# Self attention of a two-block network on one core: the causal mask moved from TensorE to VectorE and GpSimd, and the value products placed two units behind

## What is computed

```python
h = _layer_norm(x, ln1_g, ln1_b)
q, k, v = jnp.split(h @ w_qkv, 3, axis=-1)            # each B, S, 16, 16
scores = jnp.einsum('bqhd,bkhd->bhqk', q, k) * hd ** (-0.5)
causal = jnp.tril(jnp.ones((S, S), bool))
scores = jnp.where(causal, scores, jnp.finfo(scores.dtype).min)
attn = jax.nn.softmax(scores, axis=-1)
o = jnp.einsum('bhqk,bkhd->bqhd', attn, v).reshape(B, S, D)
x_resid = x + o @ w_o
```

## Time and profile before

| | |
|---|---|
| median of 3 runs | 2925.25 us (2921.18 to 2925.60) |
| span of the profiled execution | 2927.1 us, 1.85 us above the median |
| busy over the span | PE 2456.1, DVE 1872.1, POOL 1530.9, ACT 1332.9 us |
| maxima of set 0 | from 1228.3 to 1269.9 us |
| the seven sets with maxima beside them | from 1269.9 to 1563.1 us |
| last set | to 1592.2 us |

### The profile page before, as it was taken

The page is one execution under the profiler, slowest core; times in us unless marked ns, Lnnn a source line. Parts: engine busy times, 40 slices in busy tenths (PEclk is TensorE's granted clock), DMA queues, the critical chain, the costliest instruction groups (busy, mean ns, idle before and its releaser), DMA issues. The chain is left out here.

```text
span 2927.1 us, 26112 instructions
## 1 busy us (share of the span) xinstructions
PE 2456.1 (84%) x8044; PEld 1106.1 (38%) x8044; DVE 1872.1 (64%) x2521; ACT 1332.9 (46%) x2087; POOL 1530.9 (52%) x1340
## 2 busy tenths in 40 slices
PE   7989989889897788688888549999588989778978
PEld 3333323333332233333333338888332333223322
DVE  2999999999999933466663400000239999994334
ACT  4656466565664433345555212222056565542333
POOL 2999999999999811500000230000439999982010
PEclk9999999999999999899999669999689999999989
DMA  4031230321203000612310324444230320300000
GB/s 186 1 115 47 94 117 1 122 70 55 115 1 115 0 21 17 141 24 33 45 23 1 138 106 181 177 175 175 79 155 1 116 94 24 115 1 20 0 9 29
DMA packets 72193, 215.12 MB, mean 73 GB/s; under 512 B 14044, under 2 KB 39271, under 8 KB 53495
## 3 DMA queue, kind: packets, MB, share of 16 engines
q1 hardware_dynamic: 65380, 180.85, 18.9%
q10 hardware_dynamic: 3602, 24.22, 2.5%
q0 software_dynamic: 3072, 8.39, 0.9%
HBM read 187.80 MB, written 25.43 MB: 73 GB/s over the span
## 5 line engine op out<-in xcount | busy, mean ns | idle before, releaser
L895 POOL TENSOR_TENSOR s_dbu<-s_dx,s_bc 128x512 f32<-128x512 f32 x768 | 967.8, 1284 | 47.9 <-DVE s_psum L561 44.1
L480 PE MATMUL s_psum<-s_hc,ident 128*128 128x512 f32 x1536 | 832.2, 632 | 181.2 <-DVE s_hc L581 170.2
L764 ACT ACTIVATE s_psum<-s_dt,s_a_neg 128x512 f32<-128x512 f32 x768 | 521.6, 688 | 590.5 <-DVE s_hc L581 589.5
L480 PEld LDWEIGHTS s_psum<-s_hc,ident 128*128 128x128 f32 x1536 | 257.9, 192 | 695.2 <-DVE s_hc L581 505.4
L581 DVE TENSOR_TENSOR s_hc<-s_psum,s_bc 128x512 f32<-128x512 f32 x624 | 419.8, 673 | 0.6 <-PE s_psum L480 0.4
L561 DVE TENSOR_TENSOR_SCAN s_psum<-s_psum,s_state,s_dbu 128x512 f32<-128x512 f32 x312 | 395.1, 1277 | 18.5 <-ACT s_psum L764 12.7
L561 DVE TENSOR_TENSOR_SCAN s_psum<-s_psum,s_dbu 128x512 f32<-128x512 f32 x312 | 381.3, 1222 | 22.0 <-ACT s_psum L764 13.8
L1968 ACT ACTIVATE s_probs<-s_banks 128x512 f32<-128x512 f32 (+3 forms) x384 | 169.2, 493 | 149.5 <-PE s_banks L1693 107.0
L2381 POOL DMA_INDIRECT s_rows_in<-moe_out_rows,s_place x32 | 30.6, 957 | 357.0 <-DMA moe_out_rows<-s_ys 347.5
L2360 ACT ACTIVATE s_hidden<-s_banks,s_w 128x256 f32<-128x256 f32 x184 | 77.1, 470 | 300.9 <-PE s_banks L2183 300.9
L163 POOL TENSOR_TENSOR s_pair<-s_res 128x512 f32<-128x512 f32 x4 | 5.0, 1265 | 386.1 <-issue 384.6
(11 more groups left out here) (306 smaller groups left out, 3320.6 us busy)
## 6 DMA issues: line engine op xcount, KB each, us to landing
s_bc<-fwd_rows SPq DMA_DIRECT2D x64, 1024.0 KB, 4.7
s_bc<-m_rows SPq DMA_DIRECT2D x32, 1024.0 KB, 4.7
s_w<-in_moe_w SPq DMA_DIRECT2D x23, 1028.0 KB, 7.2
s_w<-in_moe_w ACTq DMA_DIRECT2D x23, 1024.0 KB, 5.5
qk_parts<-s_parts SPq DMA_DIRECT2D x48, 128.0 KB, 1.9
s_stack_q<-qk_parts SPq DMA_DIRECT2D x48, 128.0 KB, 4.5
s_stack_k<-qk_parts SPq DMA_DIRECT2D x48, 128.0 KB, 7.6
moe_in_rows<-s_zero SPq DMA_DIRECT2D x1, 5888.0 KB, 18.8
```

The costliest lines, as they stand in the source:

```text
L480: pe.matmul(psum[:, SCANS + block_no % 2, :], consts["ident"][:], hc[:, unit % PRODUCTS, :], start=(n == 0), stop=(n == NS - 1)).then_inc( ...
L764: act.activation(psum[:, unit % SCANS, :], dt[:, g % 2, i // NS, :], ACT.Exp, scale=a_neg[CHUNKS[g][0]][:, i:i + 1]).then_inc(decay_ready, 1)
L895: pool.tensor_tensor(dbu[:, unit % TERMS, :], dx[:, g % 2, i // NS, :], bc[:, 2 * n, :], ALU.mult)\
```

## The change

The mask matmuls are gone. Maxima tiles on the diagonal are reduced with `tensor_tensor_reduce`, which adds a mask tile from SBUF (`late`, now 512 columns: 384 of zeros that POOL writes, and the triangle) and takes the maximum in one statement, writing the sum back to the bank. The exponentials on the diagonal are taken without a mask, and POOL sets the forbidden ones to zero (`cut_late`, one `affine_select` for the four heads of a unit, 128 columns each); the value products of such a unit wait for POOL (`causal`) instead of ACT. Value products come two units behind the weights instead of one (`BEHIND`), so those of units 10 and 11 come in the next set, and `probs` is three units deep (`HELD`). `turn_out`, `copy_out` and `norm_heads` move accordingly.

```diff
+HELD, BEHIND = 3, 2
...
-        probs = s.sb("probs", [P, 2 * HH, CH])
+        probs = s.sb("probs", [P, HELD * HH, CH])
...
+        DIAGONAL = [t // 4 == half for t, half in UNITS]
+        def cut(q, u):
+            return q * sum(DIAGONAL) + sum(DIAGONAL[:u + 1])
...
-            sp.dma_start(late[:], dram["tri"]).then_inc(late_loaded, 16)
+            sp.dma_start(late[:, CH - P:CH], dram["tri"]).then_inc(late_loaded, 16)
...                                        # max_tile
-                if t // 4 == half:
-                    mm = pe.matmul(bank[:, w - P:w], consts["identb"][:], lateb[:, 0, :], start=False,
-                                   stop=True, skip_group_check=True)
                 mm.then_inc(max_ready, 1)
...                                        # weight_tile
-                mm = pe.matmul(bank[:, 0:w], stack_k[:, q % SLOTS, j, t * P:(t + 1) * P],
-                               stack_q[:, q % SLOTS, j, q0:q0 + w], start=True, stop=True)
-                if t // 4 == half:
-                    mm = pe.matmul(bank[:, 0:P], consts["identb"][:], lateb[:, 1, :], start=False, stop=True,
-                                   skip_group_check=True)
-                mm.then_inc(scored, 1)
+                pe.matmul(bank[:, 0:w], stack_k[:, q % SLOTS, j, t * P:(t + 1) * P],
+                          stack_q[:, q % SLOTS, j, q0:q0 + w], start=True, stop=True).then_inc(scored, 1)
...                                        # mix_heads
-                pe.wait_ge(exp_done, q * TILES + (u + 1) * HH)
+                if DIAGONAL[u]:
+                    pe.wait_ge(causal, cut(q, u))
+                else:
+                    pe.wait_ge(exp_done, q * TILES + (u + 1) * HH)
...                                        # the order on PE
-                    if u:
-                        mix_heads(q, u - 1)
-                    if q and u == 2:
+                    if u >= BEHIND:
+                        mix_heads(q, u - BEHIND)
+                    elif q:
+                        mix_heads(q - 1, NU + u - BEHIND)
+                    if q and u == 4:
                         turn_out(q - 1, 1)
-                    if u == 7:
+                    if u == 8:
                         turn_out(q, 0)
                     if q + 1 < NSETS and u == 10:
                         turn_max(q + 1)
-                mix_heads(q, NU - 1)
+            for u in range(NU - BEHIND, NU):
+                mix_heads(NSETS - 1, u)
...                                        # maxima, on DVE
-                dve.tensor_reduce(to, banks[:, i % 2, 0:w], AX.X, ALU.max).then_inc(max_read, 1)
+                if t // 4 == half:
+                    dve.tensor_tensor_reduce(banks[:, i % 2, 0:w], banks[:, i % 2, 0:w], late[:, CH - w:CH], 1.0, -3e38,
+                                             ALU.add, ALU.max, to).then_inc(max_read, 1)
+                else:
+                    dve.tensor_reduce(to, banks[:, i % 2, 0:w], AX.X, ALU.max).then_inc(max_read, 1)
...                                        # DVE, among the maxima of the next set
-                        if q and k == 17:
+                        if q and k == 26:
                             norm_heads(q - 1, 1)
-                        if k == 42:
+                        if k == 46:
                             norm_heads(q, 0)
...                                        # exp_tile and copy_out, on ACT
-                if j == 0 and unit >= 2:
-                    act.wait_ge(pv_done, unit - 1)
+                if j == 0 and unit >= HELD:
+                    act.wait_ge(pv_done, unit - HELD + 1)
-                    if q and u == 1:
+                    if q and u == 3:
                         copy_out(q - 1, 1)
-                    if u == 5:
+                    if u == 6:
                         copy_out(q, 0)
...                                        # new, on POOL, for every diagonal unit of every set
+            def cut_late(q, u):
+                pool.wait_ge(exp_done, q * TILES + (u + 1) * HH)
+                diagonal = probs[:, u % HELD * HH:(u % HELD + 1) * HH, 0:P]
+                pool.affine_select(out=diagonal, in_=diagonal, pattern=[[0, HH], [1, P]], compare_op=ALU.is_ge,
+                                   fill=0.0, base=0, channel_multiplier=-1).then_inc(causal, 1)
+            pool.memset(late[:, 0:CH - P], 0.0).then_inc(late_made, 1)
```

More of the change, by code:

```diff
@@ L1473, in self_attention @@
         w_o = s.sb("w_o", [P, KD, D])
-        late = s.sb("late", [P, 2, P])
-        lateb = s.sb("lateb", [P, 2, P], BF16)
+        late = s.sb("late", [P, CH])
         parts = s.sb("parts", [P, 2, PARTS, 4, CH], BF16)
@@ L1501, in self_attention @@
         pads_made, ones_made, late_made = s.sem("pads_made"), s.sem("ones_made"), s.sem("late_made")
+        causal = s.sem("causal")
         ready, split, split3 = s.sem("ready"), s.sem("split"), s.sem("split3")
@@ L1706, in mix_heads @@
                     mm = pe.matmul(banks[j * VW:(j + 1) * VW, 4 + half, CH - w:CH], v[:, b * QT + t, g * HH + j, :],
-                                   probs[:, u % 2 * HH + j, 0:w], start=(t == 0), stop=(t == 4 * half + 3))
+                                   probs[:, u % HELD * HH + j, 0:w], start=(t == 0), stop=(t == 4 * half + 3))
                 mm.then_inc(pv_done, 1)
@@ L1863, in _ @@
             scale_h(3)
-            dve.wait_ge(late_loaded, 16)
-            dve.tensor_copy(lateb[:], late[:]).then_inc(late_made, 1)
             for c in range(2, NCH):
@@ L1868, in _ @@
                     remainder(c, m)
+            dve.wait_ge(late_loaded, 16)
+            dve.wait_ge(late_made, 1)
             for k in range(TILES):
@@ L1964, in exp_tile @@
                 unit = q * NU + u
-                if j == 0 and unit >= 2:
-                    act.wait_ge(pv_done, unit - 1)
+                if j == 0 and unit >= HELD:
+                    act.wait_ge(pv_done, unit - HELD + 1)
                 act.wait_ge(scored, i + 1)
-                act.activation(probs[:, u % 2 * HH + j, 0:w], banks[:, WEIGHT_BANKS[i % len(WEIGHT_BANKS)], 0:w], ACT.Exp)\
+                act.activation(probs[:, u % HELD * HH + j, 0:w], banks[:, WEIGHT_BANKS[i % len(WEIGHT_BANKS)], 0:w], ACT.Exp)\
                    .then_inc(exp_done, 1)
@@ L2022, in _ @@
                 scale_res(c)
+            for q in range(NSETS):
+                for u in range(NU):
+                    if DIAGONAL[u]:
+                        cut_late(q, u)
 NSL = 256
@@ L2646, in layout @@
     tri = np.where(np.arange(P)[None] > np.arange(P)[:, None], np.float32(-1e30), np.float32(0))
-    a["tri"] = np.stack([tri, tri.T], 1)
+    a["tri"] = tri
     a["lns"] = np.stack([cols(i[f + n], KD) for n in ("ln1_g", "ln1_b", "ln2_g", "ln2_b")], 1)
```

1 line of the change is left out of this document (removed).

## The result

The changed kernel took 2929.86 us (median of 14 runs, 2925.75 to 2936.60), the kernel before on the same chip 2925.09 us (14 runs, 2919.12 to 2928.88): a ratio of 1.0021, 95% interval 1.0013 to 1.0029. It became slower, by about 6 us by the ratio and 4.8 by the two medians. I had forecast 2920.4, a gain; the number that I gave for rival (c), PE's clock, was 2929.5.

The account below looks back on a forecast made before the run. A chain of hand-overs bounds the sets, no engine being full. Six full sets −1.7, first set −2.3, first maxima −0.9, last set 0: −4.9 us from the median, 2920.4; range 2909 to 2933, the forecast's own 2916 to 2925.

Parts of the forecast that it names:

- rival (c): PE's clock: with less PE work, a second low stretch in each set costs about 1.3 us; 2929.5 us, chance 0.14.
- Sum of a set: Net of all terms in a full set of the attention: −2.46 + 1.12 + 0.57 + 0.48 = −0.29 us.
- Mask matmuls: 64 a set on PE; taking them out of the chain of hand-overs saves 2.46 us a set.
- Masked maxima: On DVE, each masked tile ends 0.08 us later; 14 such delays a set on the path: +1.12 us.
- rival (a): The masked maximum is delivered free, within the 682 ns of a reduction: −13.4 us, 2911.9 us, chance 0.22.
- (b): One delay swapped for another: 0.16 us a masked tile, +3.6 us, 2928.9 us, no measurable change; chance 0.16.
- (d): The masked maximum runs at the scan's rate: +4.7 us a set instead of +1.12, 2945 us, chance 0.08.
- Value products two behind: More product time in front of `turn_max` (+0.15 us) and low clock in units 0 and 1 (0.42): +0.57 a set.
- `norm_heads`: Moved to tile 26, it delays unit 5's fifth maximum by 0.61 us; its old place cost 0.13: net +0.48.
- POOL's mask: Eight a set, 0.65 us each, hidden until over 3 us; exposed only at the end.
- First maxima: 16 groups of three before the sets: −1.5 us from mask delays and issue, 8 × 0.08 back, −0.9 in all.
- Last set and end: After the last weight tile three units' products follow, one waiting for POOL: +0.9 us, offset by gains, put at 0.

Follow-up runs that it names:

- The halves alone: Kernel before with only the maxima masked on DVE: ratio 0.9979; changed kernel with the maxima masked by TensorE as before: ratio 0.9998.
- only_pool: Changed kernel with the maxima masked by TensorE matmuls and plain reductions as before, the rest of the change kept: 2931.78 us, ratio 0.9998.
- after_warm: Changed kernel with ten extra unread 512-column matmuls on TensorE in front of its wait for the row: 2918.17 us, ratio 0.9954.
- before_warm: Kernel before with ten extra unread 512-column matmuls on TensorE in front of its wait for the row: 2921.84 us, ratio 0.9968.
- behind2: Kernel before with only the change's order (value products two units behind, exponentials three deep, `norm_heads` moved), all mask matmuls kept: 2935.86 us, ratio 1.0007.

## Why the prediction was wrong, step by step

**The step that failed is the clock: rival (c), to which I gave 0.14, and a sum with no term for it.** I wrote that the windows "show 1.00 in every other stretch, which speaks against it". They show the kernel with its masks; what had to be asked is what holds the clock up there, and the change removes just that. One of my signs of being wrong came: a clock of 0.91 over the sets. The mechanism of (c) was nearly right: PE with less to do has more low clock. It came in another shape, not as a second stretch of 3.4 us in each set (+1.3) but as the same stretch growing to 14 to 24 us in two to five of the six later sets of a profile, at +2.8 to +6.2 each. That (c)'s 2929.5 lies 0.4 us from the median is therefore luck. The row wait starts it in most sets (the extra matmuls in the wait remove it), and the thinner work in units 0 to 3 lets it last (with 32 small matmuls there it is short). An estimate of its share in the median: seven sets at equal clock gain 7 × 0.43 = 3.0 us and the median is 5 to 6 above, so the clock takes 8 to 9 us, three sets at 2.8 or two at 4; with what the first maxima and the last set gain at equal clock (below) it is 1 to 2 us more.

The Trainium skill (TensorE: Matmul & The Clock Gate, "A second HAM failure mode: psum-queue depth-cycling") says that many short idle times between groups of matmuls can make the clock go up and down. No run here shows this mechanism: inside the stretch of 23.9 us the profile has PE busy for 23.24 us. The Trainium skill's table of states (same page, "What's actually happening") has a busy engine return to full speed; here the profile shows PE busy 4.00 of 4.00 and 9.81 of 9.90 us while the granted clock stays at 0.50 for 23.9 us. The measurement decides: at half speed the busy share in the profile doesn't tell whether the clock comes back.

The other steps, at an equal length of low clock where nothing else is said:

- **Sum of a set:** −0.29 forecast, −0.43 measured (41.67 to 41.24), −0.23 at a clock of 1.00 (40.34 to 40.11). Right, and partly by luck: by the lines below the gain was put 0.3 us too high, the costs 0.5 to 0.6 too high, and 0.2 us was lost in putting the parts together.
- **Mask matmuls:** −2.46 forecast. Those of the maxima are worth 0.65 + 0.8 = 1.5 us with 3.4 us low (1.05 at full clock, 40.34 to 39.29), those of the weights 0.75: 2.2 together.
- **Masked maxima:** +1.12 forecast, +0.79 and +0.83 measured. The accumulator read exists and has a price, which rival (a) denied; rivals (b) and (d) are out by size.
- **Value products two behind:** +0.57 forecast. The order costs 0.71 to 0.78 with `norm_heads` in it, 0.29 to 0.43 of which is `norm_heads`: +0.35 to 0.42.
- **`norm_heads`:** +0.48 forecast, 0.43 with 3.4 us low, 0.29 at full clock (40.11 to 39.82). The local wait is the +0.62 of the timeline, of which part is made up later; unit 5's part before its products is 3.52 us instead of 2.91 (1372.34 to 1375.86), the 0.6 more that I wrote.
- The halves alone give −0.65 and +0.03, the whole −0.43: 0.2 us is lost in putting them together, which I did not follow further.
- **POOL's mask:** 0.65 forecast, 0.637 measured. Its waits on PE's side come to a total of 2.4 us, 9 times, none over 0.44: in each of the seven sets a weight load of PE waits for it for 0.23 us. I had written that POOL would end no wait of PE but in the last set, which is wrong. In `only_pool` these waits leave no mark that I could find.
- **First maxima:** −0.9 forecast. The stretch cut at 1228.30 shows no gain (41.60 us for 41.61), but it doesn't begin with the work: the first maxima tile starts at 1217.62 us against 1216.88. From that tile to DVE's first row arithmetic it is 48.54 us before and 48.00 after; over all profiles with 13.7 us low in this stretch, 48.5 to 49.9 (mean 49.4 of four) with PE's mask and 47.5 to 48.8 (48.1 of five) with DVE's. So there was a gain, of 0.5 to 1.3 us.
- **First set:** −2.3 forecast; 42.26 before, 41.11 after, −1.15, though with 13.7 us low where the kernel before has 6.8. What it is at equal clock, no pair of runs shows.
- **Last set and end:** +0.9 forecast, +0.91 measured (33.65 − 32.74), and that is luck. The changed kernel has 10.2 us low in it, the kernel before 6.8. With full clock it is 30.58 us against 31.13, in `after_warm` and `before_warm`:

```profile
1553.23:1583.81 30.58, 26.34 (x190) 8.22 (x187) 2.41 (x8) 21.31 (x54) 5.71 (x9) 1.00 0.01 1
1550.76:1581.89 31.13, 27.67 (x218) 9.68 (x215) 2.42 (x8) 21.44 (x55) 0.00 (x0) 1.00 0.01 1
```

So the last set is 0.55 us shorter by the change and not 0.9 longer; the loss is the clock again.

- **Row wait:** 4.6 us forecast; `turn_max` at 1347.63, next set at 1352.26, 4.63. Units 0 and 1 together take 6.02 to 6.07 us in sets with 3.4 us low, 6.35 to 6.62 before.

## What to carry to other kernels

Work taken off TensorE can cost more than it gives when it stood just behind a wait: look in the windows at the granted clock and ask which work brings it back, before calling that work a saving. Where TensorE must stand still for a few microseconds in every round, matmuls that nobody reads, placed in the wait, were here worth more (0.3 to 0.5%) than everything the change moved. And where runs of one kernel spread by more than the effect, compare passes of equal clock inside the trace: that gave each term to 0.1 to 0.3 us, where the times of whole runs left an interval of 5 us. It holds only where the low clock is counted, not averaged away: the last set looked like a loss of 0.9 us and was a gain.

## What was not expected of the hardware

- Low stretches in later sets with the same instructions last 3.4, 13.7, 17.1 or 23.9 us. Where in the set the low clock begins goes with it (above); why, stays open.
- `behind2` has two sets at clock 1.00 with no extra matmuls and with a stand-still of 2.7 us in its row wait, as in its other sets (41.05 us). That the order of the value products does this was not tested further.
- Adding a mask and taking the maximum over 512 columns from PSUM takes 708 ns, with its accumulator read 142 ns behind it, and the next instruction starts together with that read.
- One `affine_select` over 4 × 128 columns takes 637 ns, the one over 128 columns 284 ns.
- Also open is what moves the times outside the sets: `after_warm` has runs near 2913 and near 2924 us, and its profile covers only one of the latter kind. The part behind the last set takes 1330.0 us in the changed kernel's profile and 1333.4 to 1339.6 us in the thirteen others.
